# Attention kernel on one core: the first quad's stacks copied straight from the parts, a new scratch layout, and new order tables

## Chip, core and metric

The kernel runs on one core of a Trainium2 chip. The metric is device time in microseconds (us). An execution is some 1.7 us longer than the span of its profile. The engines are TensorE (PE), VectorE (DVE), ScalarE (ACT), GpSimd (POOL) and SyncE (SP, which here only issues DMAs); they run in parallel, each in its own order, and meet at semaphores.

## What is computed

Two batches of 1024 tokens with 128 channels: a layer norm, causal attention with 16 heads of 8 channels and rotary positions, a linear layer, and the input added to both.

```python
Q, K, V = (split_heads(xn @ w.T) for w in (wq, wk, wv))      # xn = layernorm(x); 16 heads of 8
Q, K = rope(Q), rope(K)
scores = einsum('bhqd,bhkd->bhqk', Q, K) / sqrt(8)           # causal mask, softmax
out = einsum('bhqk,bhkd->bhqd', softmax(scores), V)
y = x + out @ wo.T + (xn @ CB.T) * (SCB / 127) + bias
```

## The kernel before

**Quads.** Four heads of one batch make a quad; there are 8 quads, `i` = 0 to 7. A quad is computed twice over. First come 22 *units* (`scores`, L922, into psA): query tile t of 128 rows against all its keys, whose row maxima VectorE takes (`maximum`, L796, one instruction of width 128 to 1024 for each head). Then come 36 *banks* (`shifted`, L948, into psB): scores the other way round with the maxima subtracted inside the matmul, which ScalarE exponentiates (`exps`, L691) and which 10 *steps* of `values` (L968, into psV) multiply with V. Half 0 of a quad (512 queries) has 10 banks, half 1 has 26. The maxima get into the matmul as two more rows of the query stack: GpSimd splits them (`split_maxima`), TensorE turns them (`turn_maxima`), ScalarE copies them to `shiftsT`, and a DMA (`store_shifts`, L397) puts them into `qs`.

**Stacks.** To have float32 accuracy from bf16 matmuls, each of Q and K is split into three bf16 *parts* (`part(c, n)`, n = 0, 1, 2). c = 0 to 7 counts the projections: even for Q, odd for K, two for each *round* r of 512 tokens (r = 0, 1 are batch 0, r = 2, 3 batch 1, done late). ScalarE casts part 0 (`parts_of`), VectorE takes the rest (`leave`, L766), ScalarE casts part 1, and GpSimd or VectorE subtracts for part 2 (`third_part`). `store_part` (L370) writes parts to DRAM (`q_scratch`, `k_scratch`, 8 DMAs of 128 KB a round) and `load_stack` (L384) reads them back into `qs` and `ks`, 6 DMAs of 96 KB for each half of a quad, in the order of rows that the matmul wants. A half's loads wait for all stores of its round. There are three slots of stacks, so quads 0, 1 and 2 are loaded near the start. All of this is issued by SyncE, in the order of its code.

**Tasks.** V, the linear layer and the projections of batch 1 are *tasks* (`task(n, m)`) of two halves with about 1 us of matmuls each. The first `FIRST_TASKS` = 5 stand ahead of quad 0's first unit, and the others between its units (`TASK_AFTER`: after which unit).

**Order.** The tables `UNIT_BANK`, `TURN_BANK`, `VALUE_BANK`, `SAVE_BANK` and so on say beside which bank each piece of work is issued, counted from bank 0 of the quad before (units, turns) or of the quad itself; `AHEAD` is before bank 0 of quad 0. An engine takes its instructions in that order and waits in it: a unit whose stack has not come holds up all banks behind it on TensorE.

**End.** The output of half 0 of batch 1 goes through DRAM: `save(7, 0)` (L704), `store_heads` (L404), `load_heads` (L411, L412), a reciprocal (L815), then the last projection (L1030).

## Time and profile before

| | us |
|---|---|
| time, median of 3 (lowest, highest) | 259.69 (259.62, 261.62) |
| profiled execution | 259.88 |
| its span | 258.2 |
| PE busy | 240.1 (93%) |
| DVE busy | 218.7 (85%) |
| ACT busy | 183.6 (71%) |
| POOL busy | 103.6 (40%) |

Times inside the profile count from the start of the span. Busy shares are means over a start (to about 65 us), a middle and an end (from about 225 us) that have different limits, so the prediction reads each by itself.

### The profile page before, as it was taken

The numbers are of one execution on the slowest core, as the hardware profiler recorded it, in microseconds if no ns is written. First come the engines' busy times: TensorE is split into PE (matmuls) and PEld (weight loads), VectorE is DVE, ScalarE is ACT, GpSimd is POOL, SyncE is SP. The second block draws the span as 40 slices with busy tenths as digits, with TensorE's granted clock in tenths as the row PEclk, the third lists the DMA queues.
The fourth block names the chain that finished last, engine by engine and source line by source line (L and its number), as shares of the span: only waits on it lengthen the run. The fifth ranks groups of instructions, "written<-read, shape, count | busy, mean of one in ns | idle before, by whom it ended". The sixth has DMA issues, their size and how long they took to land.

```text
span 258.2 us, 10150 instructions
## 1 busy us (share of the span) xinstructions
PE 240.1 (93%) x4294; PEld 124.1 (48%) x4294; DVE 218.7 (85%) x594; ACT 183.6 (71%) x360; POOL 103.6 (40%) x169
## 2 busy tenths in 40 slices
PE   6888896888999999999999999999999999999945
PEld 6546541233344555554554465445555554436334
DVE  7899268999999999989999998999889989962072
ACT  2045732273997888779788878889889799999701
POOL 7570724749856391293233032304401430440300
PEclk9999998699999999999999999999999999999997
DMA  7625758620230467162027103700770210010602
GB/s 196 220 66 150 202 120 156 144 46 4 67 85 23 106 165 129 44 165 67 5 81 165 29 4 103 158 18 3 192 163 5 90 41 4 3 44 20 182 10 84
DMA packets 23559, 22.96 MB, mean 89 GB/s; under 512 B 2757, under 2 KB 20549, under 8 KB 23513
## 3 DMA queue, kind: packets, MB, share of 16 engines
q1 hardware_dynamic: 23368, 22.05, 34.3%
q8 instruction: 34, 0.56, 0.9%
q10 hardware_dynamic: 144, 0.26, 0.4%
q14 instruction: 13, 0.10, 0.1%
HBM read 13.70 MB, written 8.39 MB: 86 GB/s over the span
## 4 chain that ended last, share of the span: by engine, by line
PE 72%; DVE 13%; ACT 5%; DMA 4%; SPq 2%; issue 2%; POOL 1%; ACTq 0%
PE psA L918 22%; PE psB L918 20%; PE psV L990 18%; DVE prod L802 8%; ACT ring L697 3%; PE psB L906 2%; PE psB L901 2%; PE psA L1030 2%; DMA qs<-shiftsT 2%; SPq L384 2%; DMA rest<-o_scratch 2%; PE psA L872 1%; DVE rest L815 1%; PE psB L872 1%; ACT xnT L639 1%
## 5 line engine op out<-in xcount | busy, mean ns | idle before, releaser
L802 DVE CUSTOM_DVE_ANT_0 prod<-psA,cmask 128x128 f32<-128x128 f32 (+7 forms) x256 | 177.9, 754 | 16.7 <-PE psA L918 15.6
L697 ACT ACTIVATE ring<-psB 128x512 f32<-128x512 f32 x288 | 154.5, 608 | 33.6 <-PE psB L918 30.7
L918 PE MATMUL psB<-qs,ks 128*32 128x512 bf16 (+3 forms) x1536 | 99.2, 327 | 0.5 <-DMA qs<-shiftsT 0.2
L918 PE MATMUL psA<-ks,qs 128*32 128x512 bf16 (+3 forms) x1536 | 94.7, 334 | 5.3 <-DVE mx L802 4.5
L990 PE MATMUL psV<-ring,va 128*32 128x512 f32 (+3 forms) x768 | 76.0, 486 | 0.1
L918 PEld LDWEIGHTS psB<-qs,ks 128*32 128x32 bf16 x1536 | 40.8, 96 | 48.6 <-ACT ring L697 24.2
L559 POOL TENSOR_SCALAR_AFFINE_SELECT ring<-ring 128x512 f32<-128x512 f32 x64 | 40.0, 642 | 48.2 <-ACT ring L697 48.2
L918 PEld LDWEIGHTS psA<-ks,qs 128*32 128x32 bf16 x1536 | 34.2, 96 | 43.8 <-DVE mx L802 28.0
L539 POOL CAST shifts<-mx 128x16 bf16<-128x16 f32 x16 | 3.2, 198 | 71.0 <-DVE mx L802 71.0
L990 PEld LDWEIGHTS psV<-ring,va 128*32 128x32 f32 x768 | 22.5, 110 | 16.6 <-issue 8.9
L802 DVE DVE_READ_ACCUMULATOR2_ANT mx<- 128x1 f32 x256 | 21.3, 83 | 0.0
L815 DVE RECIPROCAL rest<-rest 128x512 f32<-128x512 f32 x3 | 10.0, 3348 | 6.6 <-DMA rest<-o_scratch 6.6
L704 ACT ACTIVATE ot<-psV 128x512 f32<-128x512 f32 x16 | 9.8, 616 | 2.1 <-PE psV L990 2.0
L824 DVE TENSOR_TENSOR xn<-psA,x_sb 128x512 f32<-128x512 f32 x3 | 2.1, 692 | 7.8 <-PE psA L1030 7.8
L906 PE MATMUL psB<-w_sb,xnT 128*128 128x128 f32 x48 | 6.3, 281 | 1.8 <-ACT xnT L639 1.1
L878 PE MATMUL psA<-ident 128*128 128x128 f32 x38 | 6.0, 335 | 1.9 <-POOL ident_b L472 1.9
L639 ACT ACTIVATE xnT<-psA 128x512 f32<-128x512 f32 x2 | 1.2, 597 | 9.2 <-PE psA L866 9.2
L906 PEld LDWEIGHTS psB<-w_sb,xnT 128*128 128x128 f32 x48 | 5.7, 191 | 3.4 <-issue 1.9
L505 POOL TENSOR_TENSOR ot<-rest,ot 128x512 bf16<-128x512 f32 x3 | 3.4, 1157 | 9.3 <-ACT ot L650 9.3
L878 PEld LDWEIGHTS psA<-ident 128*128 128x128 f32 x38 | 5.8, 180 | 1.9 <-POOL ident_b L472 1.9
L901 PE MATMUL psB<-xnT,w_sb 128*128 128x512 f32 x12 | 5.8, 610 | 0.0
L748 DVE TENSOR_SCALAR xn<-x_sb,mv,rstd 128x128 f32<-128x128 f32 x16 | 5.3, 392 | 0.5 <-POOL rstd L487 0.5
(89 smaller groups left out, 157.0 us busy)
## 6 DMA issues: line engine op xcount, KB each, us to landing
qs<-q_scratch SPq DMA_DIRECT2D x48, 96.0 KB
ks<-k_scratch SPq DMA_DIRECT2D x48, 96.0 KB
o_scratch<-ot SPq DMA_DIRECT2D x12, 256.0 KB, 2.6
q_scratch<-ot SPq DMA_DIRECT2D x20, 128.0 KB, 2.5
k_scratch<-ot SPq DMA_DIRECT2D x12, 128.0 KB, 2.5
x_sb<-x SPq DMA_DIRECT2D x4, 256.0 KB, 4.5
rope_sb<-rope SPq DMA_DIRECT2D x2, 512.0 KB, 6.8
rot<-o_scratch SPq DMA_DIRECT2D x3, 256.0 KB, 3.5
```

Source lines behind the costliest of these rows:

```text
L384: sp.dma_start(stack[g * GROUP:(g + 1) * GROUP, slot, hf, :, :], source[heads, first:first + PARTS, :, tok:tok + HALF] .rearrange("h p d t ...
L559: pool.affine_select(out=view, in_=view, compare_op=ALU.is_ge, fill=0.0, base=0, pattern=[[0, QUAD], [1, P]], channel_multiplier=-1).then_ ...
L697: act.activation(ring[:, s % P_RING, k * HALF:(k + 1) * HALF], bank_b(e % B_RING), ACT.Exp)\
L704: act.activation(ot[:, i, hf * HALF:(hf + 1) * HALF], psV[:, :], ACT.Copy).then_inc(ot_saved, 1)
L748: dve.tensor_scalar(xn[:, t, :], x_sb[:, t, :], mv[:, t, 0:1], rstd[:, t:t + 1], ALU.subtract, ALU.mult).then_inc(xn_ready, 1)
L802: last = dve.tensor_tensor_reduce(masked_scores[:, u % 2, at:at + w], psA[:, (u % 2) * SEQ + at:(u % 2) * SEQ + at + w], cmask[:, SEQ - w: ...
L815: dve.reciprocal(dens[:, h % 2, :], dens[:, h % 2, :]).then_inc(dens_ready, 1)
L878: pe.transpose(bank_a(3)[:, 0:P], ident[:, :], ident[:, :])
L901: mm = pe.matmul(task_bank(n, m), w_sb[:, 2 * (c % 2) + m, :], xnT[:, (c // 2) * HALF:(c // 2 + 1) * HALF], start=True, stop=True)
L906: mm = pe.matmul(task_bank(n, m)[:, t * P:(t + 1) * P], xnT[:, at:at + P], w_sb[:, 4 if kind == "v" else 6, :], start=True, stop=True)
L918: mm = pe.matmul(psum[strip:strip + STRIP, at:at + size], keys[:, strip:strip + STRIP], queries, start=True, stop=True)
L990: mm = pe.matmul(psV[32 * j:32 * j + 32, q0:HALF], va[:, b, j, :], src, start=(s == FIRST[i][hf]), stop=(s == LAST[i][hf]))
```

## The change

- The stacks of quad 0 no longer go through DRAM. `stack_part` copies 32 partitions of each part to the stack, once for each of three groups: 12 parts, 36 DMAs from SBUF to SBUF of 32 KB, in front of all stores on SyncE's queue.
- For this the channels of a quad are permuted (`rows` in the weights and the rope table), so that the four heads of one channel lie side by side, and the scratch tensors are laid out [4 quads, parts, 8 channels, 4 heads, tokens]. A store is then described as 4 x 32 x 512 elements where it was 16 x 8 x 512; a load stays 24 x 4 x 512.
- The 16 stores of rounds 0 and 1 come after the 36 copies, then the loads of quads 1 and 2, then what was there before. The loads of quad 3 move ahead of the stores of round 3. Quad 0's two maxima DMAs are issued by ScalarE.
- Two tasks are ahead of the first unit instead of five. Rows of round 3 are turned after unit 7, with the other tasks after units 2 to 19.
- ScalarE normalises rounds 2 and 3 (GpSimd makes the bias), VectorE makes the third part of projections 1 and 3, and works on products as each matmul ends.
- All 22 units of quad 0 are ahead of bank 0, where it was 13, and the tables have new numbers.

The rows of some tables are left out here.

```diff
--- before.py
+++ after.py
-    [AHEAD, AHEAD, AHEAD, AHEAD, AHEAD, AHEAD, AHEAD, AHEAD, AHEAD, AHEAD, AHEAD, AHEAD, AHEAD, 36, 36, 36, 37, 37, 37, 39, 41, 43],
-    [8, 8, 8, 9, 9, 9, 12, 14, 15, 16, 18, 20, 21, 23, 25, 27, 28, 29, 30, 31, 32, 33],
...
+    [AHEAD, AHEAD, AHEAD, AHEAD, AHEAD, AHEAD, AHEAD, AHEAD, AHEAD, AHEAD, AHEAD, AHEAD, AHEAD, AHEAD, AHEAD, AHEAD, AHEAD, AHEAD, AHEAD, AHEAD, AHEAD, AHEAD],
+    [2, 4, 5, 6, 8, 9, 12, 13, 15, 16, 18, 19, 21, 22, 24, 26, 28, 29, 30, 32, 33, 35],
...
-    [11, 20, 22, 26, 29, 32, 35, 37, 37, 38],
+    [12, 15, 17, 21, 24, 27, 30, 37, 38, 38],
...
-    [23, 43],
+    [18, 52],
...
-PROJECT_BANK = [269, 276, 296]
-TURN_FIRST = 292
+PROJECT_BANK = [261, 271, 296]
+TURN_FIRST = 285
...
-TASKS = [("v", 0), ("ffn", 0), ("late", 4), ("late", 5), ("v", 1), ("ffn", 1), ("late", 6), ("late", 7),
-         ("max", 0)]
-FIRST_TASKS = 5
-
-TASK_AFTER = {(5, 0): 0, (5, 1): 1, (6, 0): 2, (6, 1): 2, (7, 0): 3, (7, 1): 3, (8, 0): 8}
+TASKS = [("v", 0), ("ffn", 0), ("late", 4), ("late", 5), ("max", 0), ("v", 1), ("ffn", 1), ("late", 6), ("late", 7)]
+FIRST_TASKS = 2
+
+TURN_AFTER = 7
+ROWS3_FIRST = 4
+TASK_AFTER = {(2, 0): 2, (2, 1): 2, (3, 0): 4, (3, 1): 4, (4, 0): 9, (5, 0): 9, (5, 1): 11, (6, 0): 12, (6, 1): 14, (7, 0): 15, (7, 1): 16, (8, 0): 18, (8, 1): 19}
...
-        scratch = (nc.dram_tensor("q_scratch", [HEADS, PARTS + 2, DH, BATCH * SEQ], BF16),
-                   nc.dram_tensor("k_scratch", [HEADS, PARTS, DH, BATCH * SEQ], BF16))
+        scratch = (nc.dram_tensor("q_scratch", [HEADS // QUAD, PARTS + 2, DH, QUAD, BATCH * SEQ], BF16),
+                   nc.dram_tensor("k_scratch", [HEADS // QUAD, PARTS, DH, QUAD, BATCH * SEQ], BF16))
...
-            return 16 * (2 * PARTS * (i // SLOTS + 1) + i // SLOTS)
+            n = 2 * PARTS * (i // SLOTS + 1) + i // SLOTS
+            return 16 * (n + (2 * PARTS * (PARTS - 1) if i % SLOTS == 0 else 0))
...
-                    sp.dma_start(scratch[c % 2][:, m, :, tok:tok + HALF], part(c, n)).then_inc(scratch_out[c // 2], 16)
+                    sp.dma_start(scratch[c % 2][:, m, :, :, tok:tok + HALF], part(c, n)).then_inc(scratch_out[c // 2], 16)
...
-                slot, heads, tok = i % SLOTS, slice((i % 4) * QUAD, (i % 4 + 1) * QUAD), (i // 4) * SEQ + hf * HALF
+                slot, tok = i % SLOTS, (i // 4) * SEQ + hf * HALF
                 ready = stack_in[slot][hf]
                 for g in range(PARTS):
                     for source, first, stack in ((scratch[0], g, qs), (scratch[1], 0, ks)):
                         sp.dma_start(stack[g * GROUP:(g + 1) * GROUP, slot, hf, :, :],
-                                     source[heads, first:first + PARTS, :, tok:tok + HALF]
-                                     .rearrange("h p d t -> (p d) h t")).then_inc(ready, 16)
+                                     source[i % 4, first:first + PARTS, :, :, tok:tok + HALF]
+                                     .rearrange("p d h t -> (p d) h t")).then_inc(ready, 16)
...
+            def stack_part(c, n):
+
+                hf, stack = c // 2, (qs, ks)[c % 2]
+                if n < 2:
+                    sp.wait_ge((part1, part2)[n], c + 1)
+                else:
+                    sp.wait_ge(part3[c], 1)
+                for g in range(PARTS):
+                    row = g * GROUP + ((n - g) % PARTS if c % 2 == 0 else n) * DH
+                    sp.dma_start(stack[row:row + DH, 0, hf, :, :], part(c, n)[0:QUAD * DH, :]).then_inc(stack_in[0][hf], 16)
+
+            sp.wait_ge(pads0_ready, 2)
+            for n in range(PARTS):
+                for c in (0, 1):
+                    stack_part(c, n)
+            stack_part(2, 0)
+            stack_part(2, 1)
+            stack_part(3, 0)
+            stack_part(3, 1)
+            stack_part(2, 2)
+            stack_part(3, 2)
             store_parts(0)
-            sp.wait_ge(pads0_ready, 2)
+            store_parts(1)
+            sp.wait_ge(pads1_ready, 2)
             sp.wait_ge(scratch_out[0], 16 * ROUND_DMAS)
-            load_stack(0, 0)
-            store_parts(1)
+            load_stack(1, 0)
             sp.wait_ge(scratch_out[1], 16 * ROUND_DMAS)
-            load_stack(0, 1)
-            sp.wait_ge(pads1_ready, 2)
-            load_stack(1, 0)
             load_stack(1, 1)
-            store_shifts(0, 0)
             sp.wait_ge(pads2_ready, 2)
             load_stack(2, 0)
             load_stack(2, 1)
-            store_shifts(0, 1)
             for i in range(1, QUADS):
                 store_shifts(i, ORDER[i][0])
                 if i == 1:
                     store_parts(2)
                 store_shifts(i, ORDER[i][1])
                 if i == 1:
+                    sp.wait_ge(b_filled, ring_place(i, 0))
+                    load_stack(i + 2, 0)
+                    load_stack(i + 2, 1)
                     store_parts(3)
                 for done, hf in ((i - 2, 1), (i - 1, 0)):
                     if done >= 0 and (done // 4, hf) in HALVES:
                         store_heads(done, hf)
-                if i + 2 < QUADS:
+                if 1 < i and i + 2 < QUADS:
...
+            def mean_shifts(g):
+                bt = slice(4 * g, 4 * g + 4)
+                pool.wait_ge(rstd_ready, g + 1)
+                pool.tensor_tensor(mean_shift[:, bt], mv[:, bt, 0], rstd[:, bt], ALU.mult).then_inc(shift_step, 1)
+                pool.wait_ge(shift_step, g - 1)
+                pool.tensor_scalar(mean_shift[:, bt], mean_shift[:, bt], -1.0, None, ALU.mult).then_inc(shift_ready, 1)
+
+            scales(0)
+            scales(1)
+            scales(2)
+            mean_shifts(2)
...
             third_part(0)
             third_part(2)
-            third_part(3)
-            pads(qs, 2, 0.0, pads2_ready)
-            pads(ks, 2, TWO_MINUS_ONES, pads2_ready)
+            scales(3)
+            mean_shifts(3)
...
+                    act.wait_ge(task_saved, n + 1)
+                    shift_rows = qs[SHIFT:SHIFT + NSHIFT, 0, c, :, :].rearrange("r h (t q) -> r (h t) q", q=P)
+                    act.dma_start(shift_rows, shiftsT[:, c, :]).then_inc(shift_in[c], 16)
...
+            def normalise(g):
+                act.wait_ge(shift_ready, g - 1)
+                for t in range(4 * g, 4 * g + 4):
+                    act.activation(xn[:, t, :], x_sb[:, t, :], ACT.Identity, bias=mean_shift[:, t:t + 1],
+                                   scale=rstd[:, t:t + 1]).then_inc(xn_late_ready, 1)
+
             turned_rows(0)
+            parts_of(0, 0)
             turned_rows(1)
-            for n in range(2):
-                parts_of(0, n)
-                parts_of(1, n)
+            parts_of(1, 0)
+            parts_of(0, 1)
+            parts_of(1, 1)
+            normalise(2)
+            parts_of(2, 0)
             turned_rows(2)
+            parts_of(2, 1)
+            parts_of(3, 0)
             save_task(0)
+            parts_of(3, 1)
+            for n in range(1, ROWS3_FIRST):
+                save_task(n)
+            normalise(3)
             turned_rows(3)
-            parts_of(2, 0)
-            save_task(1)
-            parts_of(3, 0)
-            parts_of(2, 1)
-            parts_of(3, 1)
-            for n in range(2, len(TASKS)):
+            for n in range(ROWS3_FIRST, len(TASKS)):
                 save_task(n)
...
+                if i == 0:
+                    act.wait_ge(exp_done, e + 1)
+                    shift_rows = qs[SHIFT:SHIFT + NSHIFT, 0, hf, :, :].rearrange("r h (t q) -> r (h t) q", q=P)
+                    act.dma_start(shift_rows, shiftsT[:, hf, :]).then_inc(shift_in[hf], 16)
...
-            rotate(0)
-            rotate(1)
+            def third_part(c):
+                dve.wait_ge(part2, c + 1)
+                dve.tensor_tensor(part(c, 2), rest[:, c % 2, :], part(c, 1), ALU.subtract).then_inc(part3[c], 1)
+
+            for c in (0, 1):
+                product(c, 0)
+                product(c, 1)
+                rotate(c)
             leave(0)
             leave(1)
-            normalise(2)
-            dve.wait_ge(part2, 2)
-            dve.tensor_tensor(part(1, 2), rest[:, 1, :], part(1, 1), ALU.subtract).then_inc(part3[1], 1)
-            normalise(3)
+            product(2, 0)
+            third_part(1)
+            product(2, 1)
             rotate(2)
+            product(3, 0)
+            leave(2)
+            product(3, 1)
             rotate(3)
-            leave(2)
             leave(3)
+            statistics(3)
+            third_part(3)
...
-                    if w % 2:
-                        mm.then_inc(projected, 1)
+                    mm.then_inc(projected, 1)
...
-                    pe.wait_ge(xnT_ready, 4 if n else 2)
+                    pe.wait_ge(xnT_ready, 2 if n == 0 else 3 if n < ROWS3_FIRST else 4)
...
             task(0, 0)
+            turn_rows(2)
             task(0, 1)
-            turn_rows(2)
-            turn_rows(3)
             for n in range(1, FIRST_TASKS):
                 for m in range(2):
                     task(n, m)
...
+                            if i == 0 and n == ROWS3_FIRST and u == TURN_AFTER:
+                                pe.wait_ge(task_saved, ROWS3_FIRST)
+                                turn_rows(3)
...
+        d = ch % (QUAD * DH) // QUAD
...
-    swap = np.arange(P) ^ 1
+    rows = np.arange(P).reshape(HEADS // QUAD, QUAD, DH).transpose(0, 2, 1).reshape(P)
+    swap = rows ^ 1
     wq, wk = np.asarray(L0_attn_wq), np.asarray(L0_attn_wk)
-    weights = np.stack([wq.T, wq[swap].T, wk.T, wk[swap].T, np.asarray(L0_attn_wv).T,
+    weights = np.stack([wq[rows].T, wq[swap].T, wk[rows].T, wk[swap].T, np.asarray(L0_attn_wv).T,
                         np.asarray(L0_attn_wo).T, np.asarray(L0_ffn_CB).T], axis=1)
```

SyncE's queue where the first stack is made. Before: the end of round 0's stores, and quad 0's first loads.

```order
L370 DMA k_scratch<-ot 16x8x512
L370 DMA q_scratch<-ot 16x8x512
L370 DMA k_scratch<-ot 16x8x512
L384 DMA qs<-q_scratch 24x4x512
L384 DMA ks<-k_scratch 24x4x512
```

After, from the middle of the copies to the first stores:

```order
L431 DMA ks<-ot 8x4x512 x3
L431 DMA qs<-ot 8x4x512 x6
L431 DMA ks<-ot 8x4x512 x6
L431 DMA qs<-ot 8x4x512 x3
L431 DMA ks<-ot 8x4x512 x3
L377 DMA q_scratch<-ot 4x32x512 x2
L377 DMA k_scratch<-ot 4x32x512
```

The stores that came first now follow 36 copies, and their leading size is 4 instead of 16.

TensorE where quad 1's first unit stands (psA 32x128 x16; psB are banks). Before:

```order
L918 MATMUL psA<-ks,qs 32x512 x8
L990 MATMUL psV<-ring,va 32x512 x4
L918 MATMUL psB<-qs,ks 32x256 x8
L918 MATMUL psA<-ks,qs 32x128 x16
L918 MATMUL psA<-ks,qs 32x256 x16
L918 MATMUL psA<-ks,qs 32x384 x8
```

After (L975 is a task):

```order
L992 MATMUL psA<-ks,qs 32x512 x8
L975 MATMUL psB<-xnT,w_sb 128x512
L992 MATMUL psA<-ks,qs 32x512 x16
L992 MATMUL psB<-qs,ks 32x512 x12
L992 MATMUL psA<-ks,qs 32x128 x16
L992 MATMUL psB<-qs,ks 32x512 x4
```

The first unit of quad 1 stood after nine banks; now it stands after three, which follow directly on quad 0's last unit and the tasks.

TensorE near the end, around step 2 of half 0 of quad 7 (psV 32x256), after which `save(7, 0)` can run. Before:

```order
L990 MATMUL psV<-ring,va 32x384 x4
L990 MATMUL psV<-ring,va 32x128 x4
L918 MATMUL psB<-qs,ks 32x512 x8
L990 MATMUL psV<-ring,va 32x256 x4
L918 MATMUL psB<-qs,ks 32x512 x8
L1030 MATMUL psA<-w_sb,rot 32x128 x16
```

After:

```order
L1106 MATMUL psA<-w_sb,rot 32x128 x16
L992 MATMUL psB<-qs,ks 32x512 x12
L1064 MATMUL psV<-ring,va 32x512 x4
L992 MATMUL psB<-qs,ks 32x512 x12
L1064 MATMUL psV<-ring,va 32x384 x4
L1064 MATMUL psV<-ring,va 32x128 x4
L992 MATMUL psB<-qs,ks 32x512 x8
L1064 MATMUL psV<-ring,va 32x256 x4
```

The step moved from bank 22 to bank 17 of the last quad, and the save from bank 23 to bank 18 (`SAVE_BANK`).

## Rows read from the trace of the kernel before

**Rows 1.** The page: the chain that ended last, shares by engine.

```profile
PE 72%; DVE 13%; ACT 5%; DMA 4%; SPq 2%; issue 2%; POOL 1%; ACTq 0%
```

**Rows 2.** Busy us of each engine (instructions), granted clock, DMA share, by stretch.

```profile
core 0: us, PE busy (x) PEld busy (x) DVE busy (x) ACT busy (x) POOL busy (x), PEclk, DMA share, GB/s
...
23.00:31.00 8.00, 7.34 (x40) 5.06 (x40) 3.57 (x6) 5.33 (x10) 3.73 (x3) 1.00 0.72 186
40.00:45.00 5.00, 2.91 (x41) 0.82 (x41) 4.96 (x15) 0.31 (x2) 2.70 (x4) 0.79 0.86 159
45.00:52.00 7.00, 6.01 (x72) 1.33 (x64) 6.69 (x15) 1.71 (x3) 5.63 (x6) 0.66 0.70 144
...
150.00:175.00 25.00, 25.00 (x507) 12.87 (x503) 23.25 (x71) 20.59 (x43) 6.21 (x14) 1.00 0.31 73
```

**Rows 3.** Timeline of DVE: units of quad 0, of quad 1, of quad 7.

```profile
31.66 0.29 DVE L802 CUSTOM_DVE_ANT_0 prod<-psA,cmask 128x128 f32<-128x128 f32 x1 [4.26 <-PE psA L918]
...
41.97 0.82 DVE L802 CUSTOM_DVE_ANT_0 prod<-psA,cmask 128x640 f32<-128x640 f32 x1
...
57.90 0.29 DVE L802 CUSTOM_DVE_ANT_0 prod<-psA,cmask 128x128 f32<-128x128 f32 x1
...
221.14 1.22 DVE L802 CUSTOM_DVE_ANT_0 prod<-psA,cmask 128x1024 f32<-128x1024 f32 x1
```

**Rows 4.** Timeline of PE: half a task (start, us, what).

```profile
31.42 1.16 PE L906 MATMUL psB<-w_sb,xnT 128*128 128x128 f32 x8
```

**Rows 5.** Chain of waits in the middle: two banks, one step of values.

```profile
120.92 0.43 PE psB L918 x8
...
122.43 0.86 PE psV L990 x8
```

**Rows 6.** Timeline of SP's DMA issues: first stores, last loads of quad 0's halves.

```profile
15.39 1.24 SPq L370 DMA_DIRECT2D q_scratch<-ot  x2
...
25.04 0.38 SPq L384 DMA_DIRECT2D ks<-k_scratch  x1
...
35.27 0.38 SPq L384 DMA_DIRECT2D ks<-k_scratch  x1
```

**Rows 7.** Issues by line: duration in ns, minimum, median, maximum.

```profile
L370 SPq DMA_DIRECT2D q_scratch<-ot x20: 517/598/1862, 15.4 to 90.8; - x20
...
DMA to landing us min/median/max: 2.3/2.5/3.6
...
L384 SPq DMA_DIRECT2D ks<-k_scratch x48: 322/376/1505, 23.4 to 187.6; - x48
...
L389 SPq DMA_DIRECT2D qs<-qs x10: 598/607/659, 95.3 to 188.0; - x10
...
L397 SPq DMA_DIRECT2D qs<-shiftsT x16: 611/634/752, 44.0 to 225.1; - x16
```

**Rows 8.** Stretches with one kind of transfer; last columns: DMA share, GB/s.

```profile
16.30:22.50 6.20, 5.54 (x30) 3.64 (x28) 6.20 (x14) 3.50 (x7) 1.65 (x2) 1.00 0.62 169
98.40:100.40 2.00, 2.00 (x41) 1.17 (x37) 2.00 (x5) 1.40 (x5) 0.00 (x0) 1.00 0.85 156
...
67.45:67.70 0.25, 0.25 (x8) 0.20 (x8) 0.25 (x3) 0.25 (x1) 0.17 (x2) 1.00 0.14 32
4.00:9.00 5.00, 4.74 (x33) 4.15 (x31) 4.56 (x21) 0.42 (x1) 3.82 (x5) 1.00 1.12 337
```

**Rows 9.** The chain of waits at the end.

```profile
237.15 0.50 ACT ot L704
...
237.66 2.23 DMA o_scratch<-ot
...
240.54 4.34 DMA rest<-o_scratch
...
249.13 1.11 PE psA L1030 x32
```

**Rows 10.** Timeline of ACT: the banks after that save.

```profile
237.48 6.36 ACT L697 ACTIVATE ring<-psB 128x512 f32<-128x512 f32 x12
```

More of the change, by code:

```diff
@@ L604, in masks @@
                         copy_v(i, 1)
[L605 to L612 removed]
+                if i == 1 and 3 <= s < 7:
+                    add_ffn(s - 3)
+                if i == 2 and 3 <= s < 7:
+                    add_bias(s - 3)
+            beside(-3)
+            pads(qs, 2, 0.0, pads2_ready)
+            pads(ks, 2, TWO_MINUS_ONES, pads2_ready)
+            for n in (-2, -1):
                 beside(n)
```

92 lines of the change are left out of this document (49 added, 43 removed), and 26 rows, old and new, of tables (UNIT_BANK, VALUE_BANK).

## The prediction

> **What bounds the kernel now.** I read the chain that ended last first: TensorE holds 72% of it and VectorE 13% [rows 1]. A table of stretches says where. From 150 to 175 us TensorE is busy for all of it and VectorE for 93% [rows 2]; the middle, from 65 to 225 us, is like that throughout. Its work has a size there: two banks take 0.43 us, a step of values 0.86 [rows 5]. A quad is 36 banks (7.7 us), as many columns of units (7.7), and 10 steps of which two are half as long (7.7): 23.2 us. Quad 0's last unit ends on VectorE at 57.9, quad 7's at 222.4 [rows 3]: 164.5 us for seven quads, 23.5 each. So the middle is TensorE's and has some 2 us of slack in all; work on VectorE, ScalarE or GpSimd there is hidden.
>
> The start is different. VectorE waits 4.26 us for the first unit, at 31.66, reaches unit 6 (the first of 640 columns) at 41.97, and then goes through the 16 long units without a pause until 57.90, where quad 1 begins [rows 3]. Between 40 and 52 us TensorE has idle time, and its clock is granted at 0.79 and 0.66 [rows 2]: TensorE waits for VectorE. The figure to follow is thus the time at which quad 1's first unit starts, 57.9 now: what it moves, the end moves, since all that follows is a full TensorE.
>
> The end has its own chain: the save of half 0 of quad 7 at 237.15, a DMA out, a DMA in, a reciprocal, and the last projection at 249.13 [rows 9], while the last 12 banks run on ScalarE from 237.48 [rows 10] and are done 5 us before that projection.
>
> **The change, part by part.**
>
> *The first stack.* Today: stores from 15.39, loads of half 0 issued until 25.4 and of half 1 until 35.65 [rows 6]. The change puts 36 copies in their place. What does the issue of one cost? The trace has no such DMA, but near ones: a store from SBUF takes 0.60 us to issue, a move from SBUF to SBUF 0.61, the maxima (SBUF to SBUF, 2 rows out of 32) 0.63; only loads from DRAM take 0.38 [rows 7]. The copies are from SBUF to SBUF, so I take 0.60 and 0.04 between two; 0.38 is the lower bound, 0.42 with the gap. The first part can be cast about 1.4 us earlier than now, since products begin at the first matmul and the cast goes ahead of a copy on ScalarE: 14.0. Half 0's 18 copies are then issued until 14.0 + 18 x 0.64 = 25.5, and with some 2.3 us to land [rows 7] TensorE can start the first unit at about 27.8, and VectorE at 28.2 instead of 31.66. Half 1's 18 end at 37.0 and land at 39.3, so unit 6 starts at about 39.5 instead of 41.97: 2.5 us earlier. (With 0.42 they would land at 31.5, and unit 6 would follow unit 5 at about 32.6.)
>
> *The tasks.* Half a task is about 1 us of TensorE [rows 4]. Four halves lie among the units of half 0, which VectorE has done at about 36, before half 1 is there; they cost nothing. Eight more lie between units 9 and 19. Ten fills of 0.3 to 0.4 us and 8 us of tasks are 11.6 us for TensorE, where VectorE needs 10.6: 1 us is lost, 1.3 with the turn of rows. So VectorE would end quad 0 at 39.5 + 15.9 (its 41.97 to 57.90 of now) + 0.3 to 1.3, which is 55.7 to 56.7: at best 2.2 us early. ScalarE's eight new normalisations take VectorE's place at it and fall in its idle time, GpSimd's four small instructions too, and VectorE's own two third parts (0.7 us each) are over before 27.8.
>
> *The stores.* This term decides. The 16 stores of rounds 0 and 1 come after the copies, from 37.0, and quad 1's stack waits for them. Now they are described as 4 x 32 x 512. How many DMA engines does a transfer use? In the stretch from 4 to 9 us, with transfers of 128 leading rows queued, the share is 1.12 (packets overlap): that is all 16. With only loads in the queue, 24 leading rows, it stays at 0.85, so 12 engines (0.85 / 1.12 x 16 = 12.1); with one maxima DMA alone, 2 leading rows, it is 0.14, so 2 engines [rows 8]. In each case it is the largest number up to 16 that divides the leading size. For 4 it is 4 engines, where the store of now, with 16, has 16. Then each engine moves 32 KB of every store. What a KB costs: 169 GB/s at a share of 0.62 is 8.9 engines and 54 ns a KB for stores; 337 GB/s on 16 is 49 ns; the loads, 156 GB/s on 12, have 79 ns [rows 8]. A store is thus 1.56 us (49 ns) to 1.73 (54 ns), at most 2.5 (79 ns); today it is bound by its issue, 0.64. I take 1.63, 26 us for 16, one after the other on the same four engines: 37.0 + 1 (issue to first packet) + 26 = 64. Round 0's are down at about 52, and the loads of quad 1 are issued, but on these four engines their packets stand behind round 1's stores; 6 x 8 KB there are 2.4 to 3.8 us. Quad 1's first half is complete at about 67.5.
>
> The Trainium skill, in "DMA: Bandwidth & Descriptors", section "Why a DMA increments its semaphore by 16 and not by 1", says that a DMA issued by SyncE or ScalarE runs on the largest k up to 16 that divides the slowest dimension of both sides. By that rule the stores have k = 4, the copies (8 and 32 rows) 8; the trace's 16, 12 and 2 agree with it.
>
> *What waits for it.* Quad 1's first unit now stands after bank 2 on TensorE, and TensorE waits in its order: banks 3 to 35 of quad 0 and their values are behind it. GpSimd, ScalarE and VectorE run dry. So nothing covers this wait: from about 56 to 67.5 TensorE stands still. Quad 1 starts at 67.5 instead of 57.9: **+9.6 us**. Half 1 of quad 1 is loaded by about 71, and needed some 6.6 us after 67.5, so it is just covered.
>
> *New places in the middle.* At quad 1's start TensorE has done 3 banks and not 9, and at quad 7's last unit (place 33, not 30) 249 instead of 246. In between it has 9 banks more, with a quarter of a quad's values: 9 x 0.215 + 1.9 = 3.8 us, of which the slack takes up to 1.9. Behind, 3 banks fewer at ScalarE's 0.53 us [rows 10] give back 1.6. Net +0.3 to +2.2, **+1.4**. The maxima of quad 1's half 1 are queued on SyncE behind the last three stores of round 2, which need 3 x 1.63 us on engines that they share; they turn at bank 39 and are needed at 46, 4.8 us later. That is 0 to 2 us late: **+1**.
>
> *The end.* Half 0 of quad 7 is saved beside bank 18 and not 23. The banks come at 0.53 us each: 5 x 0.53 = **-2.6 us** for the chain out to DRAM and back. It stays the last one: the banks' own chain would be ready about 3.8 us before the projection of now, and gets 0.9 us shorter with one step of values fewer behind the last bank.
>
> Sum against the profiled execution: 259.9 + 9.6 + 1.4 + 1 - 2.6 = 269.3; against the median, 0.2 lower: **269 us**.
>
> **Rivals.** (A) The stores use 16 engines after all, because the leading size is not what counts. For it: no transfer with a leading 4 is in the trace. It decides if 16 stores take less than 16 us in all, 1 us each, since quad 1's stack is then there before 57.9. Against it: 24 gives 12 engines, though a load's 96 rows of 1 KB could be shared out to 16. Then 16 x 0.64 us of issue end at 47.3, quad 1's loads land at about 52, and quad 1 starts at 55.7: 259.9 - 2.2 + 1.4 - 2.6 = 256.5. (B) The copies are issued in 0.38 us each, because they are small. For it: only the loads of now have as few rows an engine as they. Against it: the move of 2 rows takes 0.61. Then the stores begin at 29.1 and quad 1 is loaded at 59.6: 259.9 + 1.7 + 1.4 + 1 - 2.6 = 261.4, and slower than before only from a store of 1.5 us up. (C) Both: quad 1 starts at about 49.5, 250 us. (D) On four engines the stores run at the 79 ns a KB of the loads: 2.5 x 16 = 40 us, 282 us. Of these A and C end below the time of before.
>
> **How the numbers follow.** Forecast (264 to 276: a store of 1.5 to 1.8 us, issues of 0.60 to 0.66, the terms of the middle) 0.62; A 0.09; B 0.15 (258 to 265); C 0.04; D 0.04; the rest 0.06, a shift of the start that I don't see. A measurement can tell 1% here, 2.6 us. Faster: A mostly, C, a little of B and of the rest, 0.15. Same: most of B, some of A, 0.15. Slower: 0.70. The range of 8 in 10 leaves out C, D and the lower half of A, and a little at the edges of the rest: 257 to 276.
>
> **What would show it.** The issue of a copy: 0.60 to 0.64 us in SyncE's timeline. VectorE's first unit at about 28 and its first of 640 columns at 39.5. Stores that take over 3.5 us to land, and more the later they are issued. A DMA share near 0.28 between 42 and 52 us, where it was 0.86 and 0.70 [rows 2]. TensorE idle for some 10 us from about 56, released by a DMA into qs or ks, and at a lower clock behind it, as it was after waits before [rows 2]. The save of quad 7's half 0 some 17 banks before the last. I am wrong if the stores land in 2.5 us, or if the copies' issue is under 0.45; if quad 1 starts before 57.9, every term but the end's is.

## The result, and the profile after

The changed kernel takes 278.92 us (277.83 to 280.10, 4 runs) against 259.66 for the kernel before in the same session: ratio 1.0723, 95% interval 1.0655 to 1.079. It is slower, as forecast, but by 19 us and not by 9, and outside the range. The profiled execution took 278.6 us, with a span of 276.9. Some executions of one and the same kernel are over 1.5% longer than its fastest; a few of these lie among the runs of e8, e11 and e13 below, whose medians hold them.

**Where the time went.** VectorE's timeline of the changed kernel, at the first unit, the first of 640 columns, the first units of quads 1 and 2, and the last unit:

```profile
30.02 0.29 DVE L874 CUSTOM_DVE_ANT_0 prod<-psA,cmask 128x128 f32<-128x128 f32 x1 [3.59 <-PE psA L992]
...
42.62 0.82 DVE L874 CUSTOM_DVE_ANT_0 prod<-psA,cmask 128x640 f32<-128x640 f32 x1 [2.67 <-PE psA L992]
...
70.12 0.29 DVE L874 CUSTOM_DVE_ANT_0 prod<-psA,cmask 128x128 f32<-128x128 f32 x1 [8.76 <-PE psA L992]
...
97.28 0.29 DVE L874 CUSTOM_DVE_ANT_0 prod<-psA,cmask 128x128 f32<-128x128 f32 x1
...
244.76 1.22 DVE L874 CUSTOM_DVE_ANT_0 prod<-psA,cmask 128x1024 f32<-128x1024 f32 x1
```

Against [rows 3], the first unit is 1.6 us earlier, the first long one 0.65 us later, and quad 1 starts 12.2 us later. From there to the end of the last unit it is 175.9 us instead of 164.5, 11.4 more; behind it 30.9 us instead of 35.8, 4.9 less. 12.2 + 11.4 - 4.9 = 18.7, the difference of the spans.

**What holds up quad 1.** The chain of waits of the changed kernel, from the last copies to quad 1's maxima (SPq is time in which SyncE issues):

```profile
38.77 0.66 SPq L431
39.47 0.67 SPq L431
40.19 0.56 SPq L377
...
45.80 1.27 SPq L377
...
56.80 1.27 SPq L377
...
62.78 6.63 DMA ks<-k_scratch
69.45 0.62 PE psA L992 x16
...
72.20 6.20 DMA qs<-shiftsT
...
78.53 0.59 PE psB L992 x5
...
100.42 5.95 DMA qs<-shiftsT
```

The 36 copies fill the queue until 40.14. Then 16 stores need 17.9 us to be issued, at first at 0.56 us, then at some 1.3, as if SyncE could not put one in before an earlier one had gone on; the trace does not show the reason. The last load of quad 1's half 0 takes 6.63 us behind them. Two maxima DMAs of 8 KB take 6.20 and 5.95 us, and TensorE's timeline shows it idle before the banks that need them:

```profile
78.53 0.85 PE L992 MATMUL psB<-qs,ks 128*32 128x512 bf16 x12 [2.62 <-DMA qs<-shiftsT]
...
106.50 0.62 PE L992 MATMUL psB<-qs,ks 128*32 128x512 bf16 x4 [2.14 <-DMA qs<-shiftsT]
```

Durations of the issues by line of the changed kernel, in ns:

```profile
L431 SPq DMA_DIRECT2D qs<-ot x18: 654/655/856, 14.5 to 37.4; - x18
...
L377 SPq DMA_DIRECT2D k_scratch<-ot x12: 510/972/1392, 41.4 to 118.3; - x12
...
L391 SPq DMA_DIRECT2D ks<-k_scratch x42: 757/758/1487, 59.4 to 210.5; - x42
```

A load takes 758 ns to issue, where it was 376 [rows 7], with 24 x 4 x 512 elements both times. Only the order of the source in DRAM is another. The table of stretches, columns as in [rows 2]:

```profile
42.00:58.00 16.00, 16.00 (x157) 8.07 (x149) 12.78 (x27) 4.12 (x8) 9.82 (x9) 0.90 0.28 94
...
60.00:70.00 10.00, 0.94 (x28) 0.56 (x24) 1.36 (x4) 1.57 (x3) 0.41 (x2) 0.61 0.56 137
70.00:80.00 10.00, 7.30 (x137) 4.40 (x132) 6.83 (x33) 5.60 (x12) 5.49 (x7) 0.84 0.86 101
80.00:90.00 10.00, 9.98 (x173) 4.51 (x168) 8.17 (x19) 8.02 (x18) 6.18 (x8) 0.87 0.32 52
```

With stores in the queue the DMA share is 0.28 at 94 GB/s. TensorE stands still for 9.06 us before 69.45; the granted clock is 0.61 on average over that stretch of 10 us, and 0.84 and 0.87 over the next two. The finer stretches show two separate times at the lower of the two levels (0.50, that is 1.2 GHz) in them, one behind the wait of 9 us and one behind the maxima wait of 2.62 us, with the full clock between:

```profile
70.00:72.00 2.00, 2.00 (x44) 1.31 (x39) 1.11 (x9) 1.18 (x3) 0.64 (x1) 0.50 0.86 94
...
74.00:76.00 2.00, 1.83 (x44) 0.90 (x36) 2.00 (x9) 2.00 (x5) 0.92 (x2) 1.00 0.85 98
...
78.00:80.00 2.00, 1.47 (x24) 0.85 (x28) 0.04 (x1) 1.02 (x3) 1.92 (x2) 0.80 0.87 102
80.00:82.00 2.00, 2.00 (x24) 1.00 (x20) 0.79 (x2) 0.55 (x2) 1.92 (x5) 0.50 0.83 111
82.00:84.00 2.00, 2.00 (x44) 0.88 (x32) 1.38 (x3) 1.67 (x4) 2.00 (x3) 0.84 0.50 89
```

**The end** of the changed kernel, in the chain of waits. It is no longer the way through DRAM of [rows 9], but the last banks and values:

```profile
262.82 2.62 ACT ring L753 x5
...
265.50 1.23 POOL ring L596 x2
...
266.77 1.76 PE psV L1064 x20
```

### The profile page after: what moved, and what is told of

Its sections match the earlier page's. It is cut to its first block, busy times and chain, and to the rows that moved or that the text cites. A ratio compares the mean times of both kernels' runs of the same rounds, so it can differ in the third digit from the quotient of the medians.

```text
span 276.9 us, 10190 instructions
## 1 busy us (share of the span) xinstructions
PE 244.1 (88%) x4294; PEld 127.8 (46%) x4294; DVE 218.6 (79%) x591; ACT 187.6 (68%) x368; POOL 103.5 (37%) x168
## 4 chain that ended last, share of the span: by engine, by line
PE 64%; SPq 17%; DMA 8%; DVE 3%; issue 3%; POOL 2%; ACT 2%; POOLq 0%; DVEq 0%; ACTq 0%
PE psB L992 22%; PE psV L1064 21%; PE psA L992 19%; SPq L431 9%; SPq L377 6%; DMA qs<-shiftsT 6%; DMA ks<-k_scratch 2%; SPq L391 2%; PE psA L1106 1%; ACT ring L753 1%; POOL rstd L513 1%; POOL qs L503 1%; DVE prod L836 1%; POOL ring L596 0%; DVE xn L811 0%
## 5 line engine op out<-in xcount | busy, mean ns | idle before, releaser
L992 PE MATMUL psB<-qs,ks 128*32 128x512 bf16 (+3 forms) x1536 | 100.9, 332 | 5.2 <-DMA qs<-shiftsT 4.9
L1064 PE MATMUL psV<-ring,va 128*32 128x512 f32 (+3 forms) x768 | 78.1, 494 | 0.4 <-POOL ring L596 0.3
L992 PEld LDWEIGHTS psA<-ks,qs 128*32 128x32 bf16 x1536 | 36.7, 100 | 56.0 <-DVE mx L874 15.7
L576 POOL CAST shifts<-mx 128x16 bf16<-128x16 f32 x16 | 3.1, 196 | 79.2 <-DVE mx L874 79.2
L1064 PEld LDWEIGHTS psV<-ring,va 128*32 128x32 f32 x768 | 23.4, 112 | 17.4 <-issue 9.5
L952 PE MATMUL psA<-ident 128*128 128x128 f32 x38 | 7.1, 375 | 1.9 <-POOL ident_b L498 1.9
L975 PE MATMUL psB<-xnT,w_sb 128*128 128x512 f32 x12 | 8.0, 773 | 0.0
L584 POOL COPY va<-v_all 128x128 f32<-128x128 f32 x16 | 4.6, 290 | 8.3 <-PE psV L1064 8.3
L952 PEld LDWEIGHTS psA<-ident 128*128 128x128 f32 x38 | 6.8, 203 | 1.9 <-POOL ident_b L498 1.9
L707 ACT ACTIVATE xn<-psB 128x512 f32<-128x512 f32 x2 | 1.1, 594 | 9.2 <-PE psB L975 9.2
L513 POOL TENSOR_TENSOR rstd<-var_eps,exponent 128x4 f32<-128x4 f32 x4 | 4.5, 1124 | 6.2 <-DVE var_eps L806 6.2
L689 ACT ACTIVATE ot<-rot 128x512 bf16<-128x512 f32 x4 | 2.5, 630 | 5.8 <-DVE rot L843 5.8
```

The lines of the kernel that those rows point to most:

```text
L952: pe.transpose(bank_a(3)[:, 0:P], ident[:, :], ident[:, :])
L975: mm = pe.matmul(task_bank(n, m), w_sb[:, 2 * (c % 2) + m, :], xnT[:, (c // 2) * HALF:(c // 2 + 1) * HALF], start=True, stop=True)
L992: mm = pe.matmul(psum[strip:strip + STRIP, at:at + size], keys[:, strip:strip + STRIP], queries, start=True, stop=True)
L1064: mm = pe.matmul(psV[32 * j:32 * j + 32, q0:HALF], va[:, b, j, :], src, start=(s == FIRST[i][hf]), stop=(s == LAST[i][hf]))
```

## The experiments

Three theories to begin with. T1: the scratch layout costs, by its stores. T2: the 36 copies cost, by their 25 us of SyncE's queue. T3: late maxima transfers and the low clock cost by themselves. The time is a median; the columns behind the ratio are read from VectorE's timeline, in us from the start of the span (the starts of the first units of quads 0 to 3, and the end of the last unit). Kernels were measured in several sessions, and the ratio is to the kernel before in the same session, whose median was 259.54 (e2 to e6), 259.89 (e7 to e10), 260.59 (e11, e12) and 259.54 (e13). All kernels in one table:

| kernel | time | ratio to before (95%) | first unit | quad 1 | quad 2 | quad 3 | last unit ends |
|---|---|---|---|---|---|---|---|
| before | 259.66 | | 31.66 | 57.90 | 79.97 | 102.55 | 222.36 |
| changed | 278.92 | 1.0723 (1.0655-1.079) | 30.02 | 70.12 | 97.28 | 124.44 | 245.98 |
| e6_part_inner | 260.62 | 1.0037 (1.0006-1.0067) | 29.84 | 61.14 | 83.23 | 106.50 | 227.76 |
| e2_layout_alone | 285.05 | 1.098 (1.0918-1.1043) | 36.93 | 75.29 | 97.36 | 122.74 | 244.59 |
| e4_load_first | 279.96 | 1.0772 (1.072-1.0823) | 29.85 | 62.12 | 98.87 | 126.02 | 247.66 |
| e5_end_tables | 256.22 | 0.9864 (0.9826-0.9903) | 31.71 | 57.77 | 79.85 | 102.43 | 222.18 |
| e7_no_copies | 260.40 | 1.0033 (1.0004-1.0062) | 29.55 | 60.98 | 83.07 | 106.33 | 227.60 |
| e8_part_inner_before | 266.64 | 1.0241 (1.0176-1.0306) | 31.73 | 62.83 | 84.91 | 107.49 | 229.00 |
| e9_load_first_inner | 261.30 | 1.0055 (1.0018-1.0092) | 29.51 | 61.61 | 83.70 | 106.97 | 228.25 |
| e10_half_copies | 265.15 | 1.0205 (1.0162-1.0248) | 29.52 | 66.13 | 88.22 | 111.48 | 232.73 |
| e11_rest_alone | 256.47 | 0.9854 (0.9804-0.9904) | 28.52 | 57.31 | 79.41 | 102.67 | 223.92 |
| e12_layout_no_copies | 277.33 | 1.0681 (1.0625-1.0738) | 36.70 | 74.37 | 96.47 | 121.72 | 244.90 |
| e13_maxima_first | 286.07 | 1.1021 (1.0916-1.1125) | 29.95 | 69.32 | 92.73 | 116.00 | 249.67 |

### e6_part_inner: another order of the scratch, everything else as changed

The channels come ahead of the parts in the scratch. The 4 quads and 8 channels of a store then lie side by side in one dimension, and its leading size is 32 where it was 4. (The diffs of the experiments are shown in part.)

```diff
-        scratch = (nc.dram_tensor("q_scratch", [HEADS // QUAD, PARTS + 2, DH, QUAD, BATCH * SEQ], BF16),
+        scratch = (nc.dram_tensor("q_scratch", [HEADS // QUAD, DH, PARTS + 2, QUAD, BATCH * SEQ], BF16),
-                    sp.dma_start(scratch[c % 2][:, m, :, :, tok:tok + HALF], part(c, n)).then_inc(scratch_out[c // 2], 16)
+                    sp.dma_start(scratch[c % 2][:, :, m, :, tok:tok + HALF], part(c, n)).then_inc(scratch_out[c // 2], 16)
-                                     source[i % 4, first:first + PARTS, :, :, tok:tok + HALF]
-                                     .rearrange("p d h t -> (p d) h t")).then_inc(ready, 16)
+                                     source[i % 4, :, first:first + PARTS, :, tok:tok + HALF]).then_inc(ready, 16)
-                    row = g * GROUP + ((n - g) % PARTS if c % 2 == 0 else n) * DH
-                    sp.dma_start(stack[row:row + DH, 0, hf, :, :], part(c, n)[0:QUAD * DH, :]).then_inc(stack_in[0][hf], 16)
+                    row = g * GROUP + ((n - g) % PARTS if c % 2 == 0 else n)
+                    sp.dma_start(stack[row:row + DH * PARTS - PARTS + 1:PARTS, 0, hf, :, :], part(c, n)[0:QUAD * DH, :]).then_inc(stack_in[0][hf], 16)
```

> The changed kernel with one thing different: the DRAM scratch is ordered [quad][d][part][head][token] (a store's 128 rows then lie in 32 outer blocks, a load's source in blocks of 8), and a stack's 24 rows run (d, part) instead of (part, d). The 36 copies, all tables and orders stay. Theory T1 (the scratch layout costs): the 16 stores of rounds 0 and 1, which took 17.9 us of the DMA queue at about 1.3 us each, go back to about 0.6 us each and end near 50, load (1,0) lands near 58 to 60, quad 1 starts on VectorE near 60 instead of 70.12, quads 1 and 2 lose part of their extra 5.1 and 4.6 us: 260 to 268 us. Theory T2 (the 36 copies and their 25 us of the queue cost): copies are unchanged, stores are hidden or merely shift: 275 us or more. Theory T3 (the late maxima transfers and the low TensorE clock behind them): quad 1 starts earlier but stays 27 us long: near 270.

Measured 260.62 us, inside T1's 260 to 268: 18.3 of the 19.3 us are back, with all 36 copies in place. T1 holds, T2 and T3 fall. Its line of durations for the stores (landing after it), one for the loads, and its stretch of stores:

```profile
L377 SPq DMA_DIRECT2D k_scratch<-ot x12: 518/600/1009, 41.6 to 102.7; - x12
...
DMA to landing us min/median/max: 2.0/2.1/3.5
```

```profile
L391 SPq DMA_DIRECT2D ks<-k_scratch x42: 756/769/1279, 52.7 to 191.8; - x42
```

```profile
42.00:52.00 10.00, 10.00 (x118) 6.40 (x106) 7.80 (x17) 2.34 (x5) 9.84 (x9) 0.83 0.52 178
```

A store is issued in 0.60 us and lands in 2.1; the stretch has 0.52 at 178 GB/s where the changed kernel has 0.28 at 94. The loads of K still take 0.77 us to issue: the slow load issue is not what made the 18 us. Quads 1 and 2 take 22.1 and 23.3 us, not 27.2 each, and TensorE waits for no DMA between 60 and 140 us. e6 moves the leading size and the places in DRAM together, and no run changes one of them alone.

### e2_layout_alone: the kernel before, with the changed layout

```diff
-        scratch = (nc.dram_tensor("q_scratch", [HEADS, PARTS + 2, DH, BATCH * SEQ], BF16),
+        scratch = (nc.dram_tensor("q_scratch", [HEADS // QUAD, PARTS + 2, DH, QUAD, BATCH * SEQ], BF16),
-                    sp.dma_start(scratch[c % 2][:, m, :, tok:tok + HALF], part(c, n)).then_inc(scratch_out[c // 2], 16)
+                    sp.dma_start(scratch[c % 2][:, m, :, :, tok:tok + HALF], part(c, n)).then_inc(scratch_out[c // 2], 16)
```

> The kernel before, with the changed kernel's scratch layout alone (channels of a quad in the order d, head; the scratch [quad][part][d][head][token]; weights' rows and the rotary table in that order); no copies, tables and orders as before. T1 (layout): each store goes from about 0.57 to 1.27 us once the queue is full, so the 8 stores ahead of load (0,0) end about 5 us later, each load's issue goes from 0.38 to 0.76 us and its transfer from 79 to 122 ns/KB, so quad 0 and quad 1 both start later: 270 to 280 us, with the middle 3 us slower. T2 (copies): 259 to 262 us.

Measured 285.05 us, some 5 above T1's range and 6 slower than the changed kernel itself. T2 (259 to 262) falls. The layout alone costs 25.5 us in the old order. The chain shows the last store of each round:

```profile
20.77 8.10 DMA k_scratch<-ot
...
39.39 8.10 DMA k_scratch<-ot
```

A store lands 8.10 us after its issue, twice on the path. In [rows 7] it is 2.5.

### e4_load_first: load (1,0) ahead of round 1's stores

```diff
             store_parts(0)
-            store_parts(1)
             sp.wait_ge(pads1_ready, 2)
             sp.wait_ge(scratch_out[0], 16 * ROUND_DMAS)
             load_stack(1, 0)
+            store_parts(1)
```

> The changed kernel with the 8 stores of round 1 issued behind load (1,0) instead of ahead of it. T1: the two store rounds hold the queue for 17.9 us; load (1,0) issues some 8 us earlier, lands near 62, quad 1 starts near 62 instead of 70; but (1,1) then waits for round 1's stores, which end near 62, and lands near 72 or later, where quad 1's second half wants it near 73: 271 to 275 us. T2 (copies alone cost, start of quad 1 is not the matter): 277 to 280. T3 (late maxima transfers): less than 2 us gained, since they queue behind loads either way.

Quad 1 starts at 62.12, just as T1 said, but the time is 279.96, 5 above T1's range: nothing is gained. (That number lies in T2's and T3's ranges; e6 had already shown that neither is the cause.) Quad 1 then takes 36.75 us. TensorE's timeline shows what took the wait's place:

```profile
80.34 0.72 PE L992 MATMUL psA<-ks,qs 128*32 128x512 bf16 x8 [10.17 <-DMA ks<-k_scratch]
```

Load (1,1) now comes behind round 1's stores. The stores' time is on the path wherever they stand in front of a load that is wanted.

### e5_end_tables: the kernel before with the last quad's new numbers

```diff
-    [11, 20, 22, 26, 29, 32, 35, 37, 37, 38],
+    [12, 15, 17, 21, 24, 27, 30, 37, 38, 38],
-    [23, 43],
+    [18, 52],
-PROJECT_BANK = [269, 276, 296]
-TURN_FIRST = 292
+PROJECT_BANK = [261, 271, 296]
+TURN_FIRST = 285
```

> The kernel before with the changed kernel's tables of the last part alone: the last quad's row of the value and save tables, the places of the projection's banks and of the first turned group. In the changed kernel the time from the last unit to the end was 4.9 us shorter. If the end tables give that by themselves: 255 to 257 us. If the gain was that the end's data had lain ready longer because everything ahead was late (rival): 259 to 260 us. My prediction's term of 2.6 us: 257.

Measured 256.22 us. From the last unit's end to the end of the span it is 254.1 - 222.2 = 31.9 us, 3.9 less than before. The end's gain is real and is the tables': the kernel is 1.4% faster than before, with the interval (0.9826 to 0.9903) clear of 1.

### e7_no_copies: e6 without the copies

```diff
-            sp.wait_ge(pads0_ready, 2)
-            for n in range(PARTS):
-                for c in (0, 1):
-                    stack_part(c, n)
...
-            store_parts(0)
-            store_parts(1)
+            store_parts(0)
+            sp.wait_ge(pads0_ready, 2)
+            sp.wait_ge(scratch_out[0], 16 * ROUND_DMAS)
+            load_stack(0, 0)
+            store_parts(1)
+            sp.wait_ge(scratch_out[1], 16 * ROUND_DMAS)
+            load_stack(0, 1)
```

> The kernel of e6_part_inner without the 36 copies: quad 0 goes through the scratch as in the kernel before (stores of round 0, load (0,0), stores of round 1, load (0,1), load (1,0)), with the changed kernel's tables and order of tasks. It prices the copies in a scratch that drains on more engines. Theory T2 (the copies hold the queue until 41.7 and cost): quad 0's second half starts no later, quad 1 at 57 to 60 instead of 61.14: 257 to 260 us. Theory T1 with copies worth their issue: stores end near 21, land near 24, six loads of 0.80 us land near 31, and the first unit comes near 33 instead of 29.84; half 1's stack lands near 43 to 45 instead of 41.6; quad 1 starts near 62 to 64: 261 to 264 us.

Measured 260.40 us against 260.62: the copies are worth nothing in this layout, and neither theory's mechanism is right. The way through the scratch ends at the same times. The chain of e7, and TensorE's timeline in e6 at the same place:

```profile
38.42 3.02 DMA ks<-k_scratch
...
41.48 1.26 PE psA L983 x16
```

```profile
41.66 0.81 PE L991 MATMUL psA<-ks,qs 128*32 128x512 bf16 x12 [2.96 <-DMA ks<-ot]
```

The first unit is at 29.55 and 29.84. 36 issues at 0.70 us are as long as 16 stores, 12 loads and two landings.

### e8_part_inner_before: the kernel before with e6's layout

The same lines of the layout as in e6, put into the kernel before.

> The kernel before with the part-inner scratch layout of e6 alone (no copies, tables as before). Against e2_layout_alone (285.05 us), it changes only the order of the scratch's dimensions. T1: most of the 25 us of e2 is the stores' drain (8.1 us after the last issue, twice); here stores drain at 0.6 us each, and what is left is the load's issue, 0.67 to 0.76 us against 0.38: 6 loads ahead of each half of quads 0 and 1, 2.0 us each on the path twice: 262 to 266 us. If the loads' issue is hidden: 259 to 261. T2: unchanged from before, 259 to 260. Rival T4 (it is the loads' issue price of 0.76 us, not the stores' drain, that made e2 slow): above 275.

Measured 266.64 us, some 6.8 more than before in its session and 18.4 less than e2, just above T1's 262 to 266; T4 falls. Quad 1 starts 4.9 us later than in the kernel before, and the end is as in [rows 9].

### e9_load_first_inner and e10_half_copies: is a load still on e6's path?

e9 has e4's edit in e6. e10 is e6 with half 1 of quad 0 through the scratch: round 1's stores first, then round 0's, then the loads (0,1), (1,0), (1,1).

> The kernel of e6_part_inner with round 1's stores issued behind load (1,0). In e6 the chain from 41.6 to 58.8 is TensorE's (scores of quad 0 and the tasks of rows 2 and 3 between them), and no load is on it. If that reading is right: 260 to 261.5 us, no change or a little slower, since (1,1) lands later. If quad 1's start does wait for load (1,0): 2 to 4 us faster, 257 to 259.

> The kernel of e6_part_inner with 18 of the 36 copies: half 0 of quad 0 by copies as before, half 1 through the scratch (stores of round 1, then of round 0, then loads (0,1), (1,0), (1,1)). Each copy takes 0.70 us of the queue. The 18 copies end near 27 to 29, 16 stores at 0.64 us near 39, load (0,1) is issued by 44 and lands near 46 instead of 41.6; load (1,0) lands near 51. T1: quad 0's second half starts 4 us later, and since TensorE has tasks to do beside it, 0 to 4 us slower: 260.5 to 264.5 us. T2 (the copies' 12.6 us less of the queue count): faster, 257 to 259.

e9 measured 261.30, no change against e6: the chain of e6 is TensorE's there, not a load's. e10 measured 265.15 us, 0.65 above T1's range; T2 falls. Half 1's stack is there at 45.76, 4.1 us after e6's, and quad 1 starts 5.0 us later. So what the time follows is when half 1 of quad 0 is complete: TensorE's timeline of e10:

```profile
45.76 1.26 PE L986 MATMUL psA<-ks,qs 128*32 128x512 bf16 x16 [7.85 <-DMA ks<-k_scratch]
```

### e11_rest_alone and e12_layout_no_copies: the change's parts by themselves

e11 is the changed kernel with the old scratch layout and no copies (e7's order of the queue). e12 is the changed kernel without its copies alone.

> The changed kernel without its two parts on the scratch: the scratch layout is the old one and quad 0 comes through the scratch; the tables, the places of the tasks, the third parts and the normalisation on VectorE stay. It prices everything but layout and copies. From e7 (260.4 us, the same with the part-inner layout) with loads at 0.38 us instead of 0.67 to 0.76: if quad 1's start near 61 is TensorE's, set by the tasks of rows 2 and 3 placed among quad 0's units, nothing more is gained: 259 to 261 us. If the loads' issue still sets it, 2 to 3 us less: 256.5 to 258.5. My prediction's terms for these parts (first unit earlier, middle +1.4, end -2.6) gave 256 to 259.

> The changed kernel without its 36 copies alone: its own scratch layout, quad 0 through the scratch. Against the changed kernel (278.92 us) it prices the copies in the layout that they need; against e11 it prices the layout. T1: stores on few DMA engines drain 8.1 us behind the last issue, twice, ahead of quad 0's halves as in e2: first unit near 35, and the total near e2's, 282 to 288 us: the copies are worth 4 to 8 us there. T2 (the copies cost): below 277.

e11: 256.47 us, 1.5% faster than before. Quad 1 starts at 57.31 and not near 61: the loads' issue did set it, since e7's chain holds 12 loads of 0.67 to 0.84 us ahead of half 1 of quad 0. e11 has e5's tables in it, and its end (254.6 - 223.9 = 30.7 us) is as much shorter; it is no faster than e5, so its other parts are worth nothing that can be told. e12: 277.33 us, below T1's 282. The changed kernel has 278.92 and the two ratios' intervals overlap, so the copies gain nothing in total in their own layout either, which neither theory had. The table shows how: they do bring quad 1 forward by 4.3 us (70.12 for 74.37), but quads 1 and 2 then take 7.0 us more than e12's (27.2 and 27.2 against 22.1 and 25.3), and quad 3 takes 1.6 us less. The stretch of e12 in which only stores move, and the two drains in its chain:

```profile
39.00:47.00 8.00, 6.56 (x32) 1.81 (x30) 4.54 (x18) 3.04 (x7) 0.00 (x0) 0.81 0.25 88
```

```profile
20.06 8.41 DMA k_scratch<-ot
39.12 7.85 DMA k_scratch<-ot
```

A rival to "fewer engines" would be that each engine writes more slowly to this layout. It doesn't: 88 GB/s at a share of 0.25 are 22 GB/s for each busy engine, where the stores of before had 169 at 0.62, 17 for each [rows 8].

The kernels now divide the change's time: everything but layout and copies -3.2 us (e11 less before; -4.1 in its own session); e7's layout with the slower issue of its loads +3.9 (e7 less e11); the changed layout, whose stores are slow, +16.9 (e12 less e7; the loads of Q differ too, 0.76 us for 0.67); the copies +1.6 (changed less e12), not told from nothing. Medians of different sessions differ by up to 1 us.

### e13_maxima_first: round 2's stores behind the maxima of quad 1

```diff
                 store_shifts(i, ORDER[i][0])
-                if i == 1:
-                    store_parts(2)
                 store_shifts(i, ORDER[i][1])
                 if i == 1:
+                    store_parts(2)
```

> The changed kernel with the 8 stores of round 2 issued behind the maxima of quad 1's half 1 instead of ahead of them. In the changed kernel that maxima transfer (8 KB) takes 5.95 us from issue to landing at 100.42, right behind the last three of those stores, and TensorE idles 2.14 us for it at 106.50. Theory A (it stands behind the stores' packets on the few engines that they use): it lands in 2 to 3.5 us, the idle 2.14 us goes and so does some low clock, quad 2 starts about 3 us earlier; but the stores now end later and the maxima or loads behind them may pay: 274 to 277 us. Theory B (any small transfer is slow beside the six loads issued right behind it): it still takes 5 to 6 us, 278 to 280 us.

Theory A is right at its place: the wait of 2.14 us is gone, and quad 2 takes 23.3 us instead of 27.2, as in e6. But the time is 286.07 (four runs from 282.97 to 290.91; the profiled one is the fastest), outside both theories' ranges. The next maxima, of quad 2, now wait; SyncE's timeline, and TensorE's:

```profile
95.16 0.65 SPq L404 DMA_DIRECT2D qs<-shiftsT  x1
...
123.12 1.39 SPq L404 DMA_DIRECT2D qs<-shiftsT  x2
```

```profile
129.17 1.05 PE L991 MATMUL psB<-qs,ks 128*32 128x512 bf16 x8 [10.52 <-DMA qs<-shiftsT]
```

Between them the queue is full with 16 stores at up to 1.3 us and 12 loads at 0.80, 27 us long, longer than a quad. The maxima of quad 2 are issued at 123.12, as soon as that queue is through, where the changed kernel issues them at 122.48: what quads 1 and 2 gained is lost in front of them.

Quad 1 is shorter too, 23.4 us for 27.2, and that is not the edit's doing. Up to the last load at 79.2 us the two kernels have the same queue, and each piece is issued within 0.5 us of the same time. Even so the same loads go with a DMA share of 0.49 at 118 GB/s where the changed kernel's profile has 0.86 at 101, and the maxima of quad 0 land after 4.09 us and not 6.20, with 0.55 us of idle time and not 2.62. The chain and the stretch of e13:

```profile
71.40 4.09 DMA qs<-shiftsT
```

```profile
70.00:80.00 10.00, 9.31 (x197) 5.24 (x189) 8.71 (x35) 8.05 (x17) 6.37 (x8) 0.93 0.49 118
```

So a good part of quad 1's 27.2 us belongs to the profiled execution, or to something that no run here isolates, and not to the order of the queue.

## Why the prediction was wrong in its size

**The sign and the mechanism were right.** Its deciding term was that the stores run on 4 DMA engines, since their leading size is 4. Stores alone in the queue show a share of 0.25 at 88 GB/s (e12), which is 4 of 16; 128 KB at that rate are 1.49 us, where the forecast took 1.63. By the rule of the Trainium skill ("DMA: Bandwidth & Descriptors", "Why a DMA increments its semaphore by 16 and not by 1") k = 4, and the trace agrees. Rival A is refuted, and so are B, C and D: a copy's issue takes 0.655 to 0.672 us, and the stores did not take 2.5. (By the forecast's own terms D's sum is 283 and not 282.) TensorE did stand still for some 10 us ahead of quad 1, released by a DMA into `ks`.

**Quad 1's start**: +12.2 where +9.6 was forecast (70.1 for 67.5). The copies are issued at 0.70 us from 14.46, not at 0.64 from 14.0, and end 3.1 us later. The stores are some 0.15 us each quicker than forecast, so that round 1's are down at 64.6, where SyncE goes on to load (1,1), against 64 in the forecast. The last load of quad 1's half 0 lands 4.8 us behind them, where 3.5 was allowed, and VectorE starts another 0.7 us later. That the late end of the copies and the quicker stores nearly cancel is luck.

**The step that failed: "New places in the middle" and the maxima behind it**, +2.4 us, where +11.4 was measured. The tables are right in it: e11, which has them with the old layout, needs 166.6 us from quad 1's start to the last unit, 2.1 more than before, where +0.3 to +2.2 was said. e6, with copies and tables and quick stores, needs the same 166.6. The other 9.3 us are thus not the tables', and come only with the slow stores; quads 1 and 2 take 5.1 and 3.9 us more than in e6.
- Quad 2. The maxima of quad 1's half 1 were given 0 to 2 us, and the wait was 2.14. What was given no price is the clock behind the wait: 0.82 and 0.76 over the 4 us from 104 and the 4 from 108, which is 0.7 + 1.0 = 1.7 us of full-speed work less. 2.14 and this are 3.8, quad 2's excess. e13 shows for this pair that it is the stores in front: with them behind, quad 2 takes 23.3 us as in e6.
- Quad 1. The maxima of quad 0's half 1, moved to ScalarE's queue, don't stand in the forecast at all. They took 6.20 us, and TensorE was idle for 2.62. The forecast named "a lower clock" as a sign and gave it no price: 1.2 us less work behind the wait of 9 us, and 1.7 behind that of 2.62. Idle time and clock are 5.5, about quad 1's excess of 5.1. That these maxima share the DMA engines with the loads of quads 1 and 2 is the likely reason, but it is argued and not shown: e13's profile, with the same queue up to there, has 4.09 us and an idle time of 0.55, and e12, with the same layout and no copies, has no wait there. What made this part of the +11.4 stays open.
- The loads' issue was carried over at 0.38 us since their form was the same; it doubled. e7 against e11 prices a like rise (0.67 to 0.77 us) at 3.9 us, 3.7 of it ahead of quad 1's start and none in the middle.

**The end**: -4.9 forecast as -2.6. Only the save's place was counted (5 banks), and that term was right: in e5 the save starts 2.5 us earlier (234.53 for 237.00) and the last projection 3.0 (246.08 for 249.13). But e5 gains 3.9 us by the tables alone; most of the rest comes behind the start of that projection, to which the forecast gave nothing. The chain then turned, as the forecast had not: the banks' own chain ends last.

**Quad 0**: "1 us is lost" to the tasks on TensorE was said, 1.3 with the turn of rows, and e6 can check it. In e6 VectorE's first long unit is at 42.16 and quad 1 at 61.14, 19.0 us apart; the forecast said 16.2 to 17.2 for the changed kernel. In e11 it is 18.1. Rows of the chain there are TensorE's throughout, scores and halves of tasks by turns. In the changed kernel this was hidden under the stores.

**The first stack.** "TensorE can start the first unit at about 27.8" was 29.24, with the longer issues. That this gains something was wrong even so: e11, through the scratch, has its first unit at 28.52, before the copies' 30.02. What brought the first unit forward is most likely that two tasks stand ahead of it and not five, though no run changes that alone: before, TensorE is in tasks from 22.98 to its first unit at 31.08, and in e11 it is idle for 4.23 us until the stack lands.

Left open: why a load from the new layouts takes 0.67 to 0.77 us to issue and not 0.38, and why the loads between 70 and 80 us of the changed kernel's profile move 101 GB/s at a share of 0.86, where loads of the same form move 118 at 0.49 in e13 and 111 at 0.37 in e2.
